# Layer 0's FFN on one Trainium2 core: layer 2's folded values computed partly in front of the first tile, and one per tile behind it

## What is computed

```python
x = x + tanh(g_xattn[0]) * L0_xattn(layernorm(x), ctx)
x = x + tanh(g_ffn[0])   * L0_ffn(layernorm(x))      # the stage of this change
x = x + tanh(g_xattn[1]) * L1_xattn(layernorm(x), ctx)
...
x = x + tanh(g_xattn[2]) * L2_xattn(layernorm(x), ctx)   # 16 heads of 64
...
# layer 0's FFN; fp4() quantises blocks of 16 with one scale each
h = silu(fp4(x) @ fp4(w_gate).T) * (fp4(x) @ fp4(w_up).T)    # 256 -> 704
y = fp4(h) @ fp4(w_down).T                                    # 704 -> 256
# layer 2's attention
out = softmax(q @ k.T / 8) @ v        # per head
out = out @ w_out                     # 1024 -> 256
```

## Time and profile before

| | |
|---|---|
| Median of 3 runs | 1151.34 us (1149.43 to 1156.08) |
| The profiled execution's own time | 1153.67 us |
| Its span on the engines | 1151.9 us |
| TensorE busy over the span | 1064.0 us, 92% |
| Mean granted TensorE clock | 0.966 |
| Layer 0's FFN | 105.6 to 283.2 us |

### The profile page before, as it was taken

How to read it: one execution, slowest core, us unless ns; L and a number is a source line. 1 busy time by engine, 2 the same in 40 slices (tenths; PEclk the granted TensorE clock), 3 DMA queues, 4 the chain that set the end, 5 groups by cost and what they waited for, 6 DMA issues and landing times.

```text
span 1151.9 us, 18764 instructions
## 1 busy us (share of the span) xinstructions
PE 1064.0 (92%) x6218; PEld 906.6 (79%) x6218; DVE 795.4 (69%) x1816; ACT 518.1 (45%) x1190; POOL 165.7 (14%) x227
## 2 busy tenths in 40 slices
PE   4875799998999969998999998999979999999998
PEld 3754477776899948887888886999848888888887
DVE  5877889976888745437888875888537564565554
ACT  3465544432555545454555452566524333333222
POOL 2231000000112043221111101133214000010000
PEclk9988899999999979999999998999979999999999
DMA  9301010001000000000000005000012122121220
GB/s 288 88 1 40 1 11 1 1 1 46 29 1 0 1 11 1 1 1 1 1 1 0 1 1 233 1 0 1 1 47 65 45 68 82 53 76 47 71 82 31
DMA packets 30374, 41.19 MB, mean 36 GB/s; under 512 B 13615, under 2 KB 19577, under 8 KB 29414
## 3 DMA queue, kind: packets, MB, share of 16 engines
q1 hardware_dynamic: 29437, 39.63, 11.0%
q10 hardware_dynamic: 873, 0.72, 0.3%
HBM read 37.80 MB, written 2.54 MB: 35 GB/s over the span
## 4 chain that ended last, share of the span: by engine, by line
PE 50%; DVE 2%; ACT 1%; DMA 0%; issue 0%; DVEq 0%; POOL 0%; ACTq 0%; SPq 0%
PE psum L1937 16%; PE psum L1947 8%; PE psum L1343 6%; PE psum L1321 5%; PE psum L1164 3%; PE psum L1122 2%; PE psum L336 2%; PE psum L1331 1%; PE psum L1146 1%; PE psum L1135 1%; PE psum L1360 1%; PE psum L1909 1%; PE psum L1901 0%; PE psum L1352 0%; PE psum L1381 0%
## 5 line engine op out<-in xcount | busy, mean ns | idle before, releaser
L298 POOL TENSOR_TENSOR rstd<-ve,mhalf 128x1 f32<-128x1 f32 x128 | 82.6, 645 | 755.0 <-DVE ve L293 755.0
L347 ACT COPY work<-psum 128x256 f32<-128x256 f32 (+1 forms) x240 | 99.1, 437 | 149.4 <-PE psum L336 147.0
L336 PE MATMUL psum<-ident,work 128*128 128x128 f32 (+1 forms) x624 | 103.8, 290 | 28.6 <-DMA ctx<-in_ctx_r 8.8
L336 PEld LDWEIGHTS psum<-ident,work 128*128 128x128 f32 (+1 forms) x624 | 77.9, 150 | 45.3 <-issue 9.1
L2070 DVE TENSOR_TENSOR work<-psum,work 128x512 f32<-128x512 f32 x68 | 47.0, 691 | 85.0 <-ACT work L2007 84.8
L2010 ACT CAST h_hi<-work 128x512 fp32r<-128x512 f32 x68 | 42.2, 621 | 110.3 <-DVE work L2075 107.1
L1937 PE MATMUL psum<-x_hi,ew_hi 128*128 128x512 f32 (+1 forms) x272 | 87.4, 403 | 2.6 <-ACT work L2007 2.6
L1536 PE MATMUL psum<-early,work 128*128 128x352 f32 x256 | 83.3, 481 | 6.7 <-ACT zone L480 4.0
L1937 PE MATMUL psum<-x_lo,ew_hi 128*128 128x512 f32 (+1 forms) x272 | 84.7, 393 | 0.0
L1937 PE MATMUL psum<-x_hi,ew_lo 128*128 128x512 f32 (+1 forms) x272 | 84.5, 392 | 0.0
L1947 PE MATMUL psum<-ew_hi,h_hi 128*128 128x256 f32 x272 | 76.2, 280 | 0.8 <-DVE h_lo L2082 0.7
(11 more groups left out here) (261 smaller groups left out, 2549.3 us busy)
## 6 DMA issues: line engine op xcount, KB each, us to landing
work<-expert_shares SPq DMA_DIRECT2D x64, 256.0 KB, 3.2
early<-in_experts_in SPq DMA_DIRECT2D x1, 6528.0 KB, 18.9
x<-in_x_in SPq DMA_DIRECT2D x4, 512.0 KB, 7.1
early<-in_W_in SPq DMA_DIRECT2D x2, 1024.0 KB, 6.0
out_x<-x SPq DMA_DIRECT2D x3, 512.0 KB, 4.5
early<-in_Wk SPq DMA_DIRECT2D x1, 1024.0 KB, 6.4
early<-in_Wq SPq DMA_DIRECT2D x1, 1024.0 KB, 9.0
zone<-in_Wv SPq DMA_DIRECT2D x1, 1024.0 KB, 13.6
```

The lines of the kernel that those rows point to most:

```text
L298: pool.tensor_tensor(rstd[:, slot:slot + 1], ve[:, slot:slot + 1], mhalf[:, 0:1], ALU.pow).then_inc(s["rstd_ready"], 1)
L336: last = pe.transpose(dst[0:rows, at:at + n], src, ident[0:n, 0:n])
L347: act.copy(dst, src).then_inc(s["tr_copied"], 1)
```

## The change

The number of fold units per step becomes 4 in step -2, 2 in step -1, and 1 in each of steps 0 to 13 (before: 2 in each of steps 4 to 13). In step -2 TensorE folds before it transposes the first tile's x, and ScalarE copies those four units in its steps -4 and -3, two in each. ScalarE's copy of the first tile's transposed x moves to the head of its step -2. VectorE's count of units per two steps of its loop and SyncE's count are adapted.

```diff
-        FFN0_VALUES = 4 * 3 + 4 - 2 * 2 + 2
+        FFN0_VALUES = 4 * 3 + 4 - 2 * 2 + 2 + (4 + 2 + 3)
...
-        VO_FIRST, VO_UNITS = 4, 2
+        VO_RAMP = {-2: 4, -1: 2}
+        VO_LAST = B * KT - sum(VO_RAMP.values())

         def vo_unit(t, i):
-            n = VO_UNITS * (t - VO_FIRST) + i
+            n = i + sum(vo_units(u) for u in range(-2, t))
             return n // KT, n % KT

         def vo_units(t):

-            return VO_UNITS if not isinstance(t, int) or 0 <= t - VO_FIRST < B * KT // VO_UNITS else 0
+            return VO_RAMP.get(t, 0) if isinstance(t, int) and t < 0 else int(not isinstance(t, int) or t < VO_LAST)
...
@@ ffn0_tensor
+            def fold(t):
+                for i in range(vo_units(t)):
+                    wait(pe, s["tr_copied"], tr.n - 1)
+                    fold_values(pe, bank[TR45[tr.odd]], *vo_unit(t, i)).then_inc(s["tr_filled"], 1)
+                    tr.up()
...
+                if t == -2:
+                    fold(t)
                 if has(t + 2):
                     pe.wait_ge(s["scaled"], t + 3)
...
-                for i in range(vo_units(t)):
-                    wait(pe, s["tr_copied"], tr.n - 1)
-                    fold_values(pe, bank[TR45[tr.odd]], *vo_unit(t, i)).then_inc(s["tr_filled"], 1)
-                    tr.up()
+                if t != -2:
+                    fold(t)
...
@@ ffn0_scalar
+            def take_fold(t, units):
+                for i in units:
+                    src = bank[TR45[tr.odd]]
+                    act.wait_ge(s["tr_filled"], tr.up())
+                    take_folded_values(act, src, *vo_unit(t, i)).then_inc(s["tr_copied"], 1)
+
             def step(t, p):
+                if t == -2:
+                    take(act, s, tr, xnT[p], P, D, TR45, KD)
...
-                if has(t + 2):
+                if t in (-4, -3):
+                    take_fold(-2, (2 * t + 8, 2 * t + 9))
+                if has(t + 2) and t != -2:
                     take(act, s, tr, xnT[p], P, D, TR45, KD)
...
-                for i in range(vo_units(t)):
-                    src = bank[TR45[tr.odd]]
-                    act.wait_ge(s["tr_filled"], tr.up())
-                    take_folded_values(act, src, *vo_unit(t, i)).then_inc(s["tr_copied"], 1)
+                if t != -2:
+                    take_fold(t, range(vo_units(t)))
...
@@ ffn0_vector
-            pipeline(dve, -5, step, [(tr, 6 + 2 * VO_UNITS), (chain_n, 2 * (4 + 2 + 2))], T + 2, 5)
+            pipeline(dve, -5, step, [(tr, 6 + 2), (chain_n, 2 * (4 + 2 + 2))], T + 2, 5)
```

## The result

The changed kernel takes 1144.8 us, the median of 6 runs (1144.09 to 1146.35), against 1151.62 for the kernel before in the same session. The ratio is 0.9938, with a 95% interval of 0.9919 to 0.9958. Timed again later beside other kernels, it is 1146.63 (7 runs) against 1151.86, and 0.9941 (0.9916 to 0.9966). So it is 5 to 7 us faster. I had forecast 4.6 us less, 1146.7 us. It came out faster by more than half a percent, to which I had given 0.32.

A forecast was written before the change was run, and what follows sets the result against it. TensorE was taken to bound the kernel (92% of the span), VectorE close behind. Steps up to 3 lose 3.0 us, later steps gain 7.6: -4.6 from the median 1151.34 gives 1146.7 us, range 1142.0 to 1151.2.

The forecast's parts named there:

- later steps: Steps 4 to 13: 17 of 34 fold matmuls stay, so they take 92.4 us, 7.6 less than before.
- V(0): VectorE's product for the first tile, step 0: at 118.45 in place of 120.08, 1.6 us gained.
- G(0): Start of step 0's gate product on TensorE: forecast 120.3 against 120.66.
- G(1): Start of step 1's gate product: 129.6 at full clock or 131.05 at half clock, before 130.39.
- X(2): Start of step 2's x transposes on TensorE: forecast 149.9, before 150.03, with 1.3 us for a half clock.
- rival 2: Added folds keep TensorE warm, no gate product of steps 0 to 3 is slow: -8, 1143.3 us; chance 0.17.
- Step 2's queue: Fold copy queued behind ScalarE's 2.25 us cast: 4.4 us from x transposes to step 3's gate product, 2.5 us lost.
- G(4): Start of step 4's gate product: forecast 166.0 against 163.04, 3.0 us late.
- V(t): VectorE's product of step t's tile; TensorE's gate product was estimated to come within half a microsecond of it.
- Rival 1: Clock falls ahead of step 3's gate product, costing 1.7 us more: -2.9, 1148.4 us; chance 0.23.
- Rival 3: Queues of steps 0 to 3 cost twice the forecast and VectorE binds: 1149.7 to 1151.3 us; chance 0.09.
- rival 4: Slower: waits for VectorE put ten later gate products at half clock, +12, 1163.7 us; chance 0.06.

The follow-up runs named there:

- e4: The changed kernel without a fold unit in step 1, later units one place later and the last in step 14; 1149.94 us, 0.9967 of before.
- e5: The changed kernel without the ten fold units of steps 4 to 13, their values set to zero; those steps take 89.5 us, the stage 169.6 us.

## Why the prediction was right, and where not

The forecast was 4.6 us less with the main part, later steps, at -7.6. The stage gave 6.8 less in the first pair of traces; over all pairs of the two traces of before and the three of after it is 5.3 to 8.3. Point by point, counted from the stage's start:

- **Front.** V(0) was to be 1.6 us earlier and is (12.8 against 14.5 us); G(0) 0.4 earlier, and is 0.3. The folds in front cost nothing.
- **Steps 0 and 1.** G(1) was given as 129.6 or 131.05 by the clock, and the former came: 0.9 earlier than before, with step 0 at full clock. In the third trace the latter came (25.35 us from the start, forecast 25.4). There step 0's product was slow behind a wait of 0.46 us, so my "waits of half a microsecond never were" does not hold.
- **The step that failed** is "with the 1.3 us that a half clock cost there before, X(2) is 149.9". In the first two traces the product of step 2 ran at full clock, and X(2) was 1.8 us earlier than before, not 0.1. It was a size, not a mechanism: a product taken at 6.2 us that measured 4.90. My rival 2 had it in part. I had the clock as an unknown that falls alike before and after, and overlooked what e4 and the repeats show: a fold in step 1 leaves one slow product where there were two. In the third trace the slow one was the one of step 2, at 6.30 us, and the stage gained 5.3.
- **Step 2's queue.** 4.4 us from X(2) to G(3) was forecast, 4.31 came. X(3) to G(4): 4.4 and 4.42. G(4) is 1.2 us later than before, not 3.0. Of the 1.8 between, 1.4 is the stretch from G(2) to X(2), 7.33 us and not 8.7, 0.3 comes from G(2), as I had put X(1) between its two cases, and 0.1 is in the waits. In the third trace G(4) is 2.7 later, near the forecast. But against the second trace of before (58.9) it is 0.3 earlier in the first two: "I am wrong if G(4) is not later than before" was no fair test, as the clock alone moves G(4) by 1.5 us in either kernel.
- **Later steps.** 92.4 us forecast, 91.99 measured: -8.0 in place of -7.6. The second h unit did not have to wait for the fold copy, so a step is 9.31 and not 9.37 (8.94 with one matmul).
- **VectorE.** It did not bind, as forecast, but my limit was wrong: TensorE may come 2.1 us ahead of V(t), not half a microsecond (e5). At step 13 the gate product started 0.67 us behind V(13). I had written that 1.0 is left; my own rows give 0.7, as step 9 has one matmul.
- **Rivals.** Rival 1, a slow product in step 3, appeared in none of the traces, though TensorE waited 1.63 us ahead of it in all six in which the fold copy stood behind the cast. Against rival 2 I had said that TensorE still waits 2 us or more in each of steps 0 to 3; it waited 2.36, 2.19, 1.63 and 0.33 us. Rival 3 did not come: the queues cost what I had, and VectorE did not bind. Nor did rival 4: no product after step 2 was slow in any trace.

The forecast of -4.6, with 1.75 us more gained by G(4) and 0.4 more in the later steps, makes the -6.8 of the first pair. The median's 6.8 in the first session is the same figure, but other parts of the kernel move by 2 us between traces, and the second session gave 5.2; that the two agree so closely is partly luck.

## What to carry to other kernels

Filler work in a pipeline is priced by the step it stands in: in a stage bound by TensorE it costs its full length, in a start-up wait nothing, and behind a long instruction in another engine's queue it costs up to that instruction's time (here 1.6 us for one copy behind a cast of 2.25). When two engines are near balance, take the distance between them at the start and the difference of their periods: it tells how many steps the faster one may run before it binds. And where a kernel has waits of 2 us on TensorE, one trace is one draw of the clock. Ask first in which step a slow product costs anything (here nothing in step -1 and 1.45 us in step 0), then compare traces of the same pattern, or fill the waits.

## What the runs showed of the hardware that I had not expected

The stage ahead of this one, unchanged in all kernels, ended anywhere between 101.4 and 107.0 us in the traces, more than most effects here; lengths within a stage repeated to 0.1 us where the clock pattern was the same (170.85 and 170.77). The same gate product behind the same wait took 6.69 us in two executions and 5.00 in a third. A slow product can also follow a wait of only 0.46 us (6.44 us in step 0 of the third trace of the changed kernel). With six to twelve short bf16 matmuls in a wait, the f32 products behind it ran at full clock in both kernels in which that was tried, in one trace of each.
